# A Strassen-form matmul kernel: first x in four half-width transfers, shorter warm loop, wider VectorE sums, S2 built one product later

## The reference, cut to what matters

```
h0  = einsum('bct,bcd->bdt', x, weights[cond])        # x: (64, 64, 1024), 16 weight sets of 64x64
xf  = h0.reshape(4096, 1024)
scores = xf @ Wr.T                                    # 64 experts
G   = softmax over the 16 largest scores of a row, 0 elsewhere   # (4096, 64)
h   = einsum('nd,krd->nkr', xf, A)                    # 64 experts x rank 16 = 1024 columns
out = x + 2 * einsum('nkr,kdr->nd', h * G, B)
```

## Time and profile before

| | |
|---|---|
| median of 3 runs (lowest, highest) | 718.18 us (718.12 to 718.34) |
| profiled execution's own time | 718.08 us |
| its span in the profile | 716.3 us |
| TensorE busy | 711.7 us, 99% of the span |
| DVE, ACT, POOL busy | 479.7, 262.1, 8.4 us |
| granted clock in the profile | 1.00 throughout |

### The profile page before, as it was taken

The page is one execution under the profiler, slowest core; times in us unless marked ns, Lnnn a source line. Parts: engine busy times, 40 slices in busy tenths (PEclk is TensorE's granted clock), DMA queues, the critical chain, the costliest instruction groups (busy, mean ns, idle before and its releaser), DMA issues.

```text
span 716.3 us, 9219 instructions
## 1 busy us (share of the span) xinstructions
PE 711.7 (99%) x3436; PEld 598.9 (84%) x3436; DVE 479.7 (67%) x957; ACT 262.1 (37%) x499; POOL 8.4 (1%) x10
## 2 busy tenths in 40 slices
PE   9999999999999999999999999999999999999998
PEld 8888888888888888888888888888888888888886
DVE  4799999996537696845442868774544297788552
ACT  5576763524325431123322642132232264223200
POOL 0003000000000000000000000000000000000000
PEclk9999999999999999999999999999999999999999
DMA  9967589856886868466677676755857787546663
GB/s 327 405 227 315 167 297 396 289 225 233 299 315 214 295 214 273 175 231 219 250 250 277 248 260 202 276 182 201 281 218 248 255 313 264 183 148 199 226 223 145
DMA packets 56158, 178.41 MB, mean 249 GB/s; under 512 B 9650, under 2 KB 9778, under 8 KB 55602
## 3 DMA queue, kind: packets, MB, share of 16 engines
q1 hardware_dynamic: 54386, 174.09, 67.8%
q10 hardware_dynamic: 1728, 3.74, 1.5%
HBM read 131.66 MB, written 46.14 MB: 248 GB/s over the span
## 4 chain that ended last, share of the span: by engine, by line
PE 99%; DVE 0%; POOL 0%; issue 0%; POOLq 0%
PE Pb L248 43%; PE Pb L266 43%; PE Cb L228 7%; PE S L282 4%; PE T L521 1%; PE T L299 0%; PE T L354 0%; PE Cb L534 0%; PE S L534 0%; PE T L534 0%; DVE Q L364 0%; POOL sS L475 0%; POOLq L833 0%
## 5 line engine op out<-in xcount | busy, mean ns | idle before, releaser
L248 PE MATMUL Pb<-Op,Wt 128*128 128x512 f32 x1008 | 238.2, 392 | 0.0
L248 PEld LDWEIGHTS Pb<-Op,Wt 128*128 128x128 f32 x1008 | 187.6, 188 | 38.6 <-DVE Op L181 0.3
L266 PE MATMUL Pb<-Wt,Op 128*128 128x512 f32 x912 | 212.5, 391 | 0.0
L266 PEld LDWEIGHTS Pb<-Wt,Op 128*128 128x128 f32 x912 | 169.9, 188 | 35.1 <-DVE Op L181 0.8
L364 DVE TENSOR_TENSOR Q<-Pb,Q 128x512 f32<-128x512 f32 x112 | 77.2, 690 | 91.0 <-PE Pb L266 90.9
L266 PE MATMUL Pb<-Wt,Ox 128*128 128x512 f32 x432 | 100.8, 391 | 0.0
L266 PEld LDWEIGHTS Pb<-Wt,Ox 128*128 128x128 f32 x432 | 80.5, 188 | 16.3
L234 ACT COPY R<-Cb 128x512 f32<-128x512 f32 x60 | 35.1, 588 | 159.5 <-PE Cb L228 159.5
L181 DVE TENSOR_TENSOR Op<-R,Op 128x512 fp32r<-128x512 f32 x98 | 65.1, 688 | 19.1 <-ACT Op L179 19.1
L364 DVE TENSOR_TENSOR Cq<-Pb,Cq 128x512 f32<-128x512 f32 x64 | 43.9, 686 | 49.6 <-ACT Cq L375 30.9
L248 PE MATMUL Pb<-Ox,Wt 128*128 128x512 f32 x288 | 66.3, 389 | 0.0
(11 more groups left out here) (85 smaller groups left out, 427.8 us busy)
## 6 DMA issues: line engine op xcount, KB each, us to landing
Wt<-Wd SPq DMA_DIRECT2D x168, 512.0 KB, 4.9
Wd<-Wt SPq DMA_DIRECT2D x56, 512.0 KB, 3.9
Q<-in_x SPq DMA_DIRECT2D x32, 512.0 KB, 5.1
xc<-in_x SPq DMA_DIRECT2D x24, 512.0 KB, 3.9
out<-Q SPq DMA_DIRECT2D x32, 256.0 KB, 2.5
out<-Q SPq DMA_DIRECT2D x16, 512.0 KB, 2.8
BR<-in_B SPq DMA_DIRECT2D x3, 1024.0 KB, 8.4
BR<-in_x SPq DMA_DIRECT2D x11, 256.0 KB, 11.0
```

Of the source, the lines that this page charges most:

```text
L248: t = pe.run(lambda e, c=c, o=o, a=a, z=z: e.matmul(Pb[:, b, :], Wt[:, k, a, 128 * c:128 * c + 128], part(o, z), start=fresh and (c, a, z) ...
L266: t = pe.run(lambda e, c=c, o=o, k=k, a=a, z=z: e.matmul(Pb[:, b, :], part(o, a)[:, 128 * i:128 * i + 128], Wt[:, k, z, :], start=fresh an ...
```

## The change

The first x (columns 512 to 1023 of blocks 0 to 3) came in four transfers of one block each, three from SP and one from ACT, with rows of 2 KB. Now each of four transfers brings 256 columns of two blocks (rows of 1 KB), two from SP and two from ACT, all ahead of the transfers of A; the first two blocks c of y21 need only the first pair. `Wr` and `ident` are loaded later, `ident` from SP. The registers are loaded by DVE when `cond` has landed, before it waits for the weight sets and the cleared `wbd`. WARM goes from 22 to 15. T1, T3, T4 and part of A's sums become single DVE instructions over two or four blocks. T3 of B moves from POOL to DVE, recorded at step (5, 1) of sweep 0's first half. S2 (`S2g`) is recorded in product 1 of the second half, right ahead of its split.

```diff
-WARM = 22
+WARM = 15
...
+            ve.after(cn)
+            ve.run(numbers, False)
             ve.after(*tokens)
-            ve.run(numbers, False)
...
+        def load_x1(lane, k, b):
+
+            l = l_x0[2 * k + b][1]
+            x1_ready[k][b] = lane.load(l, lambda e: e.dma_start(
+                raws[k].rearrange("p (i a) n -> p i a n", a=2)[:, :, 1, 256 * b:256 * b + 256],
+                xf[256 * k:256 * k + 256, 512 + 256 * b:768 + 256 * b].rearrange("(i p) n -> p i n", p=128)))
...
-        load_x0(sp, 0, 1)
-        load_x0(sp, 1, 1)
-        load_x0(ac, 2, 1)
-        load_x0(sp, 3, 1)
+        for b in range(2):
+            load_x1(sp, 0, b)
+            load_x1(ac, 1, b)
         load_an(ac, 0, 1)
...
-        t_id = ac.load(l_id, lambda e: e.dma_start(idn[:, :], ident[:, :]))
...
-                pe.after(wbd_ready[i], x0_ready[i][1])
+                pe.after(wbd_ready[i], x1_ready[i // 2][c // 2])
...
-            def sum_t1(c):
-                t1[c] = add(ve, y11[c], y12[c], y11[c], split["y11"][c][1], R_ready[1][0], op=ALU.subtract)
+            def sum_t1():
+                t1[:] = [add(ve, rows(0, 0, 4), rows(2, 0, 4), rows(0, 0, 4), *[split["y11"][c][1] for c in range(4)],
+                             R_ready[1][0], op=ALU.subtract)] * 4
...
-                                raw["T3b", c] = add(gp, BR[:, 1, c, :], BR[:, 2, c, :], BR[:, 1, c, :], B_ready[1],
-                                                    B_ready[2], op=ALU.subtract)
...
+                        if s == 0 and j == 1:
+                            t = add(ve, BR[:, 1, :, :], BR[:, 2, :, :], BR[:, 1, :, :], B_ready[1], B_ready[2],
+                                    op=ALU.subtract)
+                            raw.update({("T3b", c): t for c in range(4)})
...
                         Cq_ready[0][c] = add(ve, q[0], q[0], q[1], Cq_ready[0][c], Cq_ready[1][c])
-                        raw["S2g", c] = add(ve, s2_place(c), q[0], q[3], Cq_ready[0][c], Cq_ready[3][c],
-                                            *((u_busy[c],) if s else (split["y22"][c][1], t2[c], t3[c])),
-                                            op=ALU.subtract)
                     elif m < 6:
+
+                        if m == 1:
+                            raw["S2g", c] = add(ve, s2_place(c), q[0], q[3], Cq_ready[0][c], Cq_ready[3][c],
+                                                *((u_busy[c],) if s else (split["y22"][c][1], t2[c], t3[c])),
+                                                op=ALU.subtract)
                         need(uses[m + 1], c)
```

More of the change, by code:

```diff
@@ L477, in adaln_ffn @@
         x0_ready = [[None, None] for _ in range(8)]
+        x1_ready = [[None, None] for _ in range(2)]
         an_ready = [[None, None] for _ in range(8)]
@@ L502, in adaln_ffn @@
         load_an(sp, 3, 1)
-        t_wr = ac.load(l_wr, lambda e: e.dma_start(SG[:, 0, :], Wr))
-        t_id = ac.load(l_id, lambda e: e.dma_start(idn[:, :], ident[:, :]))
         for i in range(4):
             load_x0(sp, i, 0)
+        t_wr = ac.load(l_wr, lambda e: e.dma_start(SG[:, 0, :], Wr))
         load_an(ac, 0, 0)
@@ L514, in adaln_ffn @@
         load_an(ac, 3, 0)
-        for a in range(2):
-            for i in range(4, 8):
-                load_x0(sp, i, a)
+        for i in range(4, 8):
+            load_x0(sp, i, 0)
+        t_id = sp.load(l_id, lambda e: e.dma_start(idn[:, :], ident[:, :]))
+        for i in range(4, 8):
+            load_x0(sp, i, 1)
         pe.after(z_s)
@@ L525, in a_unit @@
             made[m, j] = unit(4 * m + j, a_source(m, j), *tokens, free=free, bank=bank)
-        cond_first(0, cn, t_wa, z_w)
+        cond_first(0, t_wa, z_w)
         banks = [Cb[:, 0, :], Cb[:, 1, :], S[:, :], T[:, :, :].rearrange("p a n -> p (a n)")]
@@ L563, in adaln_ffn, with rows @@
             y11, y21, y12, y22 = [[R[:, k // 2, 4 * (k % 2) + c, :] for c in range(4)] for k in range(4)]
-            def sum_t1(c):
-                t1[c] = add(ve, y11[c], y12[c], y11[c], split["y11"][c][1], R_ready[1][0], op=ALU.subtract)
+            def rows(k, lo, hi):
+                return R[:, k // 2, 4 * (k % 2) + lo:4 * (k % 2) + hi, :]
+            def sum_t1():
+                t1[:] = [add(ve, rows(0, 0, 4), rows(2, 0, 4), rows(0, 0, 4), *[split["y11"][c][1] for c in range(4)],
+                             R_ready[1][0], op=ALU.subtract)] * 4
@@ L568, in sum_t2, with sum_t3 @@
             def sum_t2(c):
                 t2[c] = add(ve, y11[c], y22[c], y11[c], split["T1"][c][1], R_ready[1][1], op=ALU.subtract)
[L571 to L581, removed]
+            def sum_t3():
+                t3[:] = [add(ve, rows(2, 0, 4), rows(3, 0, 4), rows(2, 0, 4), *[split["y12"][c][1] for c in range(4)],
+                             R_ready[1][1], op=ALU.subtract)] * 4
@@ new lines, in sum_t4, with sums_a @@
+            def sum_t4(lo, hi):
+                t4[lo:hi] = [add(ve, rows(1, lo, hi), rows(1, lo, hi), rows(0, lo, hi),
+                                 *[split["y21"][c][1] for c in range(lo, hi)], *t2[lo:hi], R_ready[0][1],
+                                 op=ALU.subtract)] * (hi - lo)
+            def sums_a(lo, hi):
+                A11, A12 = Q[:, lo:hi, 0:512], Q[:, lo:hi, 512:]
+                A21, S1 = Q[:, lo + 4:hi + 4, 0:512], Cq[:, 2, lo:hi, :]
+                k = range(lo, hi)
+                t = add(ve, A21, A11, A21, *[raw["S1", j] for j in k], *[an_ready[j][0] for j in k], op=ALU.subtract)
+                raw.update({("S3", j): t for j in k})
+                t = add(ve, A11, S1, A11, t, *[made[1, j] for j in k], op=ALU.subtract)
+                raw.update({("S2", j): t for j in k})
+                t = add(ve, A12, A12, A11, t, *[made[0, j] for j in k], op=ALU.subtract)
+                raw.update({("S4", j): t for j in k})
@@ L632, in adaln_ffn @@
                             a_unit(2, j, raw["S1", j])
-                            for k in ((1,), (2, 3), (), ())[j]:
-                                sums_a(k)
+                            if j < 2:
+                                sums_a(*((1, 2), (2, 4))[j])
                             if j == 3:
@@ L649, in adaln_ffn @@
                         if s == 0 and j == 3:
-                            sums_a(0)
+                            sums_a(0, 1)
                         if s and j == 3:
-                            for c in range(4):
-                                sum_t1(c)
+                            sum_t1()
                     elif m == 1:
@@ L663, in adaln_ffn @@
                         sum_t2(j)
-                        if s == 0 and j == 3:
-                            for c in range(4):
-                                raw["T3b", c] = add(gp, BR[:, 1, c, :], BR[:, 2, c, :], BR[:, 1, c, :], B_ready[1],
-                                                    B_ready[2], op=ALU.subtract)
                     elif m == 3:
@@ L674, in adaln_ffn @@
                         if j == 1:
-                            for c in range(4):
-                                sum_t3(c)
+                            sum_t3()
                         if s == 0:
@@ L679, in adaln_ffn @@
                         if s and j == 3:
-                            for c in range(4):
-                                sum_t4(c)
+                            sum_t4(0, 4)
                     elif m == 4:
@@ L685, in adaln_ffn @@
                         if s == 0 and j > 1:
-                            sum_t4(2 * j - 4)
-                            sum_t4(2 * j - 3)
+                            sum_t4(2 * j - 4, 2 * j - 2)
                         if s:
```

## The result

The changed kernel takes 719.37 us in the median (719.10 to 720.39, 13 runs) against 718.21 of the kernel before in the same comparison: a ratio of 1.0017, 95% interval 1.0009 to 1.0024. It is slower by 0.17%. The forecast was 717.4, and the range ended at 718.7.

A forecast was written before the change was run, and what follows sets the result against it. TensorE, busy 711.7 of 716.3 us, was taken to bound the kernel. From 718.18 the terms -1.14 - 0.17 - 0.20 - 0.31 + 1.06 = -0.76 gave 717.4 us, range 716.2 to 718.7.

The forecast's parts named there:

- The head: Start up to L248: seven fewer warm matmuls give -1.54, A0 landing later costs +0.4, so -1.14 us.
- The halved rows of x: First x transfers, 1 KB rows: an estimated 4.5% more DMA time, some 0.1 us, not in the sum.
- Rival B: Start: x or A comes late enough that the head gains nothing; 718.6, or 718.7 with A0 later; chance 0.18.
- The wait for S2: Sweep 0, product 1, step (1, 3): DVE-ACT-DVE hop makes a load late by 1.18, net +1.06 us; none in later sweeps.
- rivals A and C: A: no new S2 wait, 716.4, chance 0.22. C: S2 wait in all four sweeps, 720.6, chance 0.08.
- the price of T3 of B on DVE: Sweep 0's first half, step (5, 1): the sum of at most 2.49 us on DVE is covered, priced at 0.
- a bound of 2.4 us: T3 of B on DVE: the most it would cost if the cover were gone.
- the wait near 61: L248's wait for a DVE low part stretched by POOL's sums: goes once T3 leaves POOL, -0.17 us.
- the one near 110: L266's wait in the stretch at 108.52: goes because DVE leaves sweep 0's first half less behind, -0.20 us.
- G11's wait: Wait at 125.4 for G11's low part of block 3: goes with S2 out of product 0, -0.31 us.
- joined sums: T1, T3, T4 and A's sums on DVE: can only get shorter, by at most a few tenths; no term in the sum.

The follow-up runs named there:

- head alone: The kernel before with only the changed cond_first, loads and 15 warm matmuls, no other edit: 717.05 us against 718.38.
- both edits back: The changed kernel with T3 of B on POOL and S2 in product 0 again: 716.88 us against 718.38 for the kernel before.
- all three mends: The changed kernel with T3 of B early on DVE (step (3, 1)), S2 one step ahead, A0 on SP: 716.25 us, ratio 0.9968 to the kernel before.

## Why the prediction was wrong

**The head was right.** Forecast -1.14, measured -1.3 (head alone, 718.38 to 717.05). That L248 stood in its profile within 0.06 of the forecast is in part luck: the first real load came 0.16 later than forecast (7.07), and A0 held L248 back by about 0.1 and not by 0.35. Over the nine profiles with 15 warm matmuls L248 started between 10.65 and 11.60, in eight of them by 11.05; forecast was 10.83. The halved rows of x cost nothing that can be told from this scatter. Rival B (no gain in the head) did not happen.

**The wait for S2 was right in place, cause and size.** Forecast a wait of 1.18 on the load side and +1.06 net. The profile shows 1.08; the two kernels that differ in S2 alone with T3 on POOL differ by 717.76 - 716.88 = 0.9 us, though their intervals overlap. With T3 on DVE the difference is 719.37 - 718.47 = 0.9 us too, and there the intervals lie apart (by the ratios 1.3 us), so the sign is sure and the size good to a few tenths. The hop took 1.38 where I had 1.43. It came in sweep 0 alone, so rivals A and C fall as well.

**The step that failed is the price of T3 of B on DVE.** I priced it at 0, with two covers: that the drain behind it had 3.6 us to spare, and that DVE would come out of the first half 1 to 2 us less behind because POOL no longer stretched it. The first was true and beside the point: the drains met their banks, and no load waited for a bank. But a lag on an engine without idle time is not used up by the nearest cover; it travels to the tightest one. I had the tightest in my hands. The wait of 0.3 on G12's low part near 110 said that there was no slack at all, and before DVE had no rest between 57 and 128 us. I did name a bound of 2.4 us, but it went into neither a rival nor the range. The second cover was wrong: the stretch was removed at 58 to 66 us, and DVE spent what it won idling at ACT's casts from 62 to 74. ACT itself was waiting there for TensorE, as its timeline in the changed kernel shows:

```profile
69.06 0.59 ACT L293 COPY sS<-S 128x512 f32<-128x512 f32 x1 [2.86 <-PE S L282]
...
72.22 0.37 ACT L302 COPY sc<-T 128x256 f32<-128x256 f32 x1 [0.53 <-PE T L299]
```

The casts that DVE waits for stand behind these copies of PE's results, and what DVE gains there does not bring these results of TensorE forward. Taking T3 of B off POOL and putting it on DVE was forecast at -0.17 for the wait near 61 and -0.20 for the one near 110, -0.37 in all. The runs show +1.6 (716.88 to 718.47 with the sum moved, 1.55 alone in the kernel before; by the ratios of the changed kernel and the one with T3 back 1.8). The single terms, and the -0.31 for G11's wait, can be told only from profiles: the waits near 61 and 125 are missing in the changed kernel, the one near 110 has grown to 1.86, and a new one of 0.26 stands near 99.

**The sum again.** Head -1.3, joined sums -0.2 (within the noise), T3 of B +1.6, S2 +0.9 (forecast -0.31 + 1.06 = +0.75): -1.3 - 0.2 + 1.6 + 0.9 = +1.0 us in all, measured +1.2. The forecast had -0.37 where T3 of B now has +1.6, and that alone carries 717.4 to 719.4.

## What to carry to other kernels

Time taken off an engine is worth something later only if that engine has no idle time in between; look for the next instruction that waits for something the freed engine does not drive. Price a new instruction on a saturated engine against the tightest consumer downstream until its next idle gap, not against the next one, and put it into such a gap: here the same sum cost 1.6 us at a full place and left no wait behind it in a gap. Where a sum is moved next to its consumer on another engine, count the round trip (0.7 us of idling a step here) and record it one step ahead.

## What the runs showed of the hardware

The time at which the passes of the warm loop sped up differed from one execution to the next. In the changed kernel's profile the warm loads before 5.9 us look like this:

```profile
L530 PEld LDWEIGHTS T<-sS x22: 289/333/338, 1.3 to 5.8; 128*128 128x128 f32 x22
```

At 333 ns they are 0.21 us apart; later ones take 192 ns and are 0.11 apart. The spacing halves, as it would between the two levels of TensorE's clock, 1.2 and 2.4 GHz, but the profile gives a granted clock of 1.00 all along, so that the clock is the reason is inferred and not shown. With the same 15 matmuls, begun at 1.32 us each time, the first real load stood at 6.62 us in one profile and at 7.36 in another, from the timelines of the kernels with both edits back and with T3 on POOL:

```profile
6.62 1.87 PEld L543 LDWEIGHTS Cb<-wbd,BR 128*128 128x128 f32 x16
```

```profile
7.36 1.87 PEld L543 LDWEIGHTS Cb<-wbd,BR 128*128 128x128 f32 x16
```

That is 0.7 us of scatter between executions that no edit made. The prediction took one moment of it, from one profile, as fixed. The two kernels with all three mends scatter least: 716.21 to 716.40 over six runs with 15 warm matmuls, 715.88 to 716.18 with 12. In the profile of the second L248 waited for A0, in that of the first it did not; why both scatter so little was not tried.

Four joined 128x512 sums of VectorE took 2.29 us in one instruction against 2.49 in four: joining saves 0.07 us for each of the three instructions that it does away with. One by one they are 0.68 us long and start 0.60 apart, so they overlap.
